# A fused attention and mixture-of-experts kernel: q's high part taken two steps earlier, one residual addition later, weight loads behind the value copies, and three waits of GpSimd left out

## The chip, the cores and the metric

The kernel runs on 1 core of one Trainium2 chip. The metric is the device time of one execution in microseconds (us); lower is better. One execution of the kernel before was also taken by the hardware profiler, and every row below is from that execution.

## The reference

The input x has 4 batches of 512 rows of 256 numbers. Everything is float32.

```python
x = x + attention(layernorm(x), W_qkv, W_out, s)
x = x + experts(layernorm(x), gating_w, w1, b1, w2, b2)

# attention: 8 key/value heads, 4 query heads for each, head size 64
q, k, v = split(layernorm(x) @ W_qkv)
q, k = rope(q), rope(k)            # only a quarter of each head really turns
attn = q @ k.T / 8, masked with -inf where 0 <= q_pos - k_pos < 64
w = softmax([attn, sink s])[..., :-1]
out = (w @ v) @ W_out

# experts: 8, the top 2 for each token, 640 places in each
gates = softmax(x_flat @ gating_w); top 2, normalised
buf[expert, place] = x_flat[token]
h = relu(buf @ w1 + b1); out_e = h @ w2 + b2
out[token] += weight * out_e[expert, place]
```

## The kernel before, in words

**Periods.** The attention is cut into 32 groups: one key/value head of one batch each, with its four query heads. A group has 16 units, one query head times 128 query rows against all 512 keys. The code runs in periods of 16 steps, one unit in a step. `all_periods` (L382) goes through the steps for each engine and calls `step(n, g, j)` four times in each: with n from 0 to 15 for the period's own group, with n - 16 for the group after it, with n + 16 for the group before it and with n + 32 for the one before that. So n = -8 of the next group lies at step 8 of this period, and n = 33 of a group lies at step 1, two periods on. The tables at L357 to L376 say at which n something is done. Every engine runs its own list in this order and stops at any wait that is not met.

**Exact products.** The float32 operands of the matrix products are taken apart in a high part (rounded by ScalarE) and a low part (the difference, by GpSimd), and each product is the sum of three.

**What is done for one group.** In the order of its numbers n:

- TensorE (PE) makes three chunks of the projection: KV (keys and values), Q01 and Q23 (two query heads each). ScalarE (ACT) copies each to `chunk_sb` (`chunk_out`, L879).
- SyncE (SP) copies the quarters that turn against one another into `swap_sb` with two or four DMAs (`swap_halves`, L514).
- GpSimd (POOL) multiplies both with the tables (`turn_parts`, L696 and L698) and adds them (`sum_parts`, L707). ACT takes the high part (`high_part`, L901: `k_hi`, `q_hi`), and POOL the low one (`low_part`, L716: `k_lo`, `q_lo`). For Q23 this is in the group's own period, at step 1 (turn), 2 (sum) and 4 (high and low), and PE needs it for unit 8. For KV and Q01 it is in the second half of the period before.
- The keys' parts are copied to the other 64 partitions by SP (L520, L525). PE turns the values (`turn_v`), ACT copies them to `v_next` (`v_copy`, L887), and SP takes them through DRAM into `v_quads` (`v_out` L532, `v_in` L540).
- In each unit PE makes the scores (L1605), VectorE (DVE) masks them and finds the maximum (L1203), ACT takes the exponentials (L914), and DVE transposes two units at once (L1212, three steps behind the first of them).
- In the next period PE multiplies with the values at steps 4, 6 and 8 (L1631), and DVE divides by the sums (L1232, `heads_sb`). The reciprocals of the sums go through DRAM on SP (`recip_out` L548, `recip_spread` L556, into `recip_wide`). PE multiplies with the output weights (L1663), ACT takes this to `y_sb`, and POOL adds it to x in two halves, the residuals (L750), at n = 33 and 42.
- SP loads the projection weights of the group after the next in three DMAs (`load_w`, L501, L503, L505). ACT and POOL split them (L907, and L663: `w_lo`).

**What else lies in the periods.** In periods 2 to 9 ACT issues a DMA of 662.5 KB that fills one expert's rows in DRAM (L986). In periods 3, 4, 5, 6, 8, 9, 13 to 17 and 22 a tile of 128 rows of a later batch is normalised: ACT writes it at step 2 (L1048), PE turns it at step 4, after ACT's copy of chunk Q01 at step 3; ACT takes its high part at step 5 (L869) and DVE its low part, also at step 5 (L1195). From period 8 on, the batch before is routed to its experts; this is `route`, at numbers r that go on over 8 periods. There POOL computes some small tiles, and at r = 92, 99, 108, 115 and 124 it scatters rows to DRAM (`indirect_dma_start`, L805). r = 99 and 115 are step 3 of the 7th and 8th period of a batch, and each scatter first waits until the reciprocals of a group have landed in `recip_wide`.

Behind the 32 periods, the last batch is routed and the 8 experts run. The change leaves their lists as they are.

## Time and profile before

| | us |
|---|---|
| the runs: median of 3 | 1124.78 |
| the runs: lowest and highest | 1120.2 and 1127.68 |
| the profiled execution | 1124.78 |
| its span in the trace | 1123.0 |
| mean granted TensorE clock, share of full speed | 0.972 |

The span is from the first to the last instruction that the profiler recorded, and the execution's own time is 1.78 us longer. The profiled execution is the median one. Busy times are sums over the instructions of an engine. In a row of a timeline, the first two numbers are start and duration in us; a bracket at its end gives how long the engine had been idle and what released it.

### The profile page before, as it was taken

To read this page: it belongs to the slowest core of one execution; us is meant where nothing else is said; L and a number is where in the kernel's file an instruction comes from. 1 tells how busy PE (TensorE), PEld (TensorE's weight loads), DVE (VectorE), ACT (ScalarE), POOL (GpSimd) and SP (SyncE) were. 2 spreads that over 40 slices of the span, in tenths; PEclk is the share of its full clock that TensorE was granted. 3 is DMA by queue.
4 is the path that set the end of the run, shared out by engine and by line. 5 is a ranking of instruction groups with operands and counts; after the bars stand their busy time and mean duration, and the time that the engine had idled before them with its cause. 6 is when DMAs were issued, how large, how long until landed. Compare 5 with 4: busy or idle time off the path is not lost.

```text
span 1123.0 us, 33679 instructions
## 1 busy us (share of the span) xinstructions
PE 1022.2 (91%) x13525; PEld 791.3 (70%) x13525; DVE 924.3 (82%) x1964; ACT 725.5 (65%) x1796; POOL 753.1 (67%) x671
## 2 busy tenths in 40 slices
PE   6799988899999789999998899999878999999996
PEld 4476666676667566777766567776556899999995
DVE  6898888799999877999997699999784677777773
ACT  4776667677787766778876577877563445445541
POOL 5677777777888779887887788888762233333332
PEclk8899999999999998999999899999899999999999
DMA  4454444445333333344333345344324344444331
GB/s 109 112 123 120 113 118 124 121 131 138 100 89 99 90 94 94 85 122 103 80 94 92 93 109 134 85 108 101 97 63 133 120 120 118 114 101 102 98 77 20
DMA packets 118061, 116.27 MB, mean 104 GB/s; under 512 B 35760, under 2 KB 104432, under 8 KB 117776
## 3 DMA queue, kind: packets, MB, share of 16 engines
q1 hardware_dynamic: 100128, 94.36, 30.8%
q0 software_dynamic: 7296, 8.55, 4.7%
q10 hardware_dynamic: 10480, 11.20, 3.6%
q8 instruction: 107, 1.75, 0.7%
q14 instruction: 50, 0.41, 0.1%
HBM read 74.84 MB, written 21.83 MB: 86 GB/s over the span
## 4 chain that ended last, share of the span: by engine, by line
PE 40%; DVE 23%; POOL 12%; DMA 7%; issue 6%; SPq 5%; ACT 5%; ACTq 0%; POOLq 0%; DVEq 0%
PE bank L1796 10%; DVE probs_ring L1203 10%; PE bank L1631 9%; DVE probs_t L1212 8%; PE bank L1807 6%; PE bank L1605 4%; PE bank L1810 3%; DMA swap_sb<-chunk_sb 3%; DMA recip_wide<-recip_rows 3%; POOL chunk_sb L707 3%; POOL swap_sb L698 3%; SPq L514 3%; ACT probs_ring L914 2%; PE bank L1548 2%; DVE heads_sb L1232 2%
## 5 line engine op out<-in xcount | busy, mean ns | idle before, releaser
L914 ACT ACTIVATE probs_ring<-probs_ring,neg_max 128x512 f32<-128x512 f32 x512 | 365.8, 717 | 182.9 <-DVE neg_max L1203 179.7
L1203 DVE CUSTOM_DVE_ANT_0 probs_ring<-bank,mask,sink_neg 128x512 f32<-128x512 f32 x512 | 359.3, 736 | 42.3 <-PE bank L1605 41.3
L1212 DVE STREAM_TRANSPOSE probs_t<-probs_ring 128x1024 f32<-128x1024 f32 x256 | 318.0, 1242 | 12.7 <-ACT probs_ring L914 12.7
L1631 PE MATMUL bank<-probs_t,v_quads 32*64 32x256 f32 x8192 | 256.3, 391 | 0.2
L1631 PEld LDWEIGHTS bank<-probs_t,v_quads 32*64 32x64 f32 x8192 | 183.5, 136 | 56.1 <-issue 30.0
L1605 PE MATMUL bank<-k_hi,q_hi 64*128 64x512 f32 x512 | 129.6, 497 | 67.5 <-POOL q_lo L716 32.1
L845 POOL DMA_INDIRECT out<-expert_sb,slots x40 | 77.4, 1936 | 154.1 <-DVE expert_sb L1475 132.8
L696 POOL TENSOR_TENSOR chunk_sb<-chunk_sb,rope_sb 128x512 f32<-128x512 f32 (+1 forms) x94 | 120.6, 1283 | 47.3 <-DMA swap_sb<-chunk_sb 40.0
L1605 PEld LDWEIGHTS bank<-k_hi,q_hi 64*128 64x128 f32 x512 | 49.9, 187 | 137.4 <-DVE neg_max L1203 52.2
L1122 ACT ACTIVATE hidden<-bank,b_sb 128x320 f32<-128x320 f32 x128 | 60.4, 524 | 110.7 <-PE bank L1796 107.8
L707 POOL TENSOR_TENSOR chunk_sb<-chunk_sb,swap_sb 128x512 f32<-128x512 f32 (+1 forms) x94 | 120.4, 1281 | 2.6
L698 POOL TENSOR_TENSOR swap_sb<-swap_sb,rope_sb 128x512 f32<-128x512 f32 (+1 forms) x94 | 120.5, 1282 | 0.0
L1663 PE MATMUL bank<-wo_sb,heads_sb 64*128 64x256 f32 x992 | 117.2, 376 | 0.0
L1807 PE MATMUL bank<-w_part,hidden_hi 128*128 128x512 f32 x320 | 114.9, 400 | 0.0
L1605 PE MATMUL bank<-k_lo,q_hi 64*128 64x512 f32 x512 | 105.5, 401 | 0.0
L1605 PE MATMUL bank<-k_hi,q_lo 64*128 64x512 f32 x512 | 105.0, 399 | 0.0
L1663 PEld LDWEIGHTS bank<-wo_sb,heads_sb 64*128 64x128 f32 x992 | 95.1, 186 | 13.9
L914 ACT ACTIVATION_READ_ACCUMULATOR probs_ring<-probs_ring,neg_max 128x1 f32 x512 | 97.4, 190 | 0.0
L1810 PE MATMUL bank<-w_part,hidden_lo 128*128 128x256 f32 x320 | 90.1, 282 | 0.0
L1548 PE MATMUL bank<-xcur,w_hi 64*128 64x512 f32 x496 | 84.9, 408 | 5.4 <-ACT y_sb L923 3.4
L716 POOL TENSOR_TENSOR q_lo<-chunk_sb,q_hi 128x512 fp32r<-128x512 f32 x63 | 80.6, 1280 | 6.4 <-ACT q_hi L901 6.2
L1796 PE MATMUL bank<-slots_hi,w_hi 128*128 128x320 f32 x256 | 79.5, 311 | 2.6 <-ACT hidden L1122 2.6
(202 smaller groups left out, 1813.7 us busy)
## 6 DMA issues: line engine op xcount, KB each, us to landing
v_quads<-v_rows SPq DMA_DIRECT2D x128, 128.0 KB
recip_wide<-recip_rows SPq DMA_DIRECT2D x64, 256.0 KB, 4.7
w_raw<-in_L_ffn_w SPq DMA_DIRECT2D x14, 1024.0 KB, 8.8
swap_sb<-chunk_sb SPq DMA_DIRECT2D x314, 32.0 KB, 3.2
w_raw<-in_L_attn_W_qkv SPq DMA_DIRECT2D x31, 256.0 KB, 2.9
slots<-slot_rows SPq DMA_DIRECT2D x9, 662.5 KB, 4.0
slot_rows<-xn ACTq DMA_DIRECT2D x8, 662.5 KB, 6.5
v_rows<-v_next SPq DMA_DIRECT2D x32, 128.0 KB, 2.1
```

What stands on the lines that cost most here:

```text
L696: nc.gpsimd.tensor_tensor(chunk_sb[c][rows, :], chunk_sb[c][rows, :], rope_sb[rows, 0, :], ALU.mult).then_inc(s_pool, 1)
L698: nc.gpsimd.tensor_tensor(swap_sb[c][rows, :], swap_sb[c][rows, :], rope_sb[rows, 1, :], ALU.mult).then_inc(s_pool, 1)
L707: nc.gpsimd.tensor_tensor(chunk_sb[c][rows, :], chunk_sb[c][rows, :], swap_sb[c][rows, :], ALU.add).then_inc(s_rot, 1)
L914: nc.scalar.activation(probs[(g * UNITS + n) % RING][:, :], probs[(g * UNITS + n) % RING][:, :], ACT.Exp, bias=neg_max[j][:, n:n + 1], sca ...
L1203: nc.vector.tensor_tensor_reduce(probs[(g * UNITS + n) % RING][:, :], SCORE[SCORE_OF[n // 2][n % 2]][:, :], mask[:, L - P - t * P:2 * L - ...
L1212: nc.vector.transpose(probs_t[j][:, :, (h // 2) * (2 * P):(h // 2 + 1) * (2 * P)] .rearrange("p b (h q) -> p h b q", h=2)[:, :, :, t * BLK ...
L1605: ins = nc.tensor.matmul(SCORE[SCORE_OF[n // 2][hh]][:, :], q[half, t * P:(t + 1) * P], k[half, :], start=(m == 0), stop=(m == 2))
L1631: ins = nc.tensor.matmul(PV[a][p * HD:(p + 1) * HD, 0:2 * P], v_quads[j][rows, d, c * HD:(c + 1) * HD], probs_t[j][rows, blk, p * 2 * P:(p ...
L1663: ins = nc.tensor.matmul(PV[a][:, 0:D], heads_sb[rows, a, h * P:(h + 1) * P], wo_sb[rows, (g % NKV) * 2 + h, :], start=(half == 0 and h == ...
L1796: ins = nc.tensor.matmul(banks[4 + 2 * (c % 2) + half][:, 0:HALF], w[:, kc, c * P:(c + 1) * P], a[:, at:at + HALF], start=(kc == 0 and m = ...
L1807: nc.tensor.matmul(FFN2[s][:, :], hidden_hi[:, c, s * P:(s + 1) * P], w2_parts[e % 2][:, c, :, :].rearrange("p t d -> p (t d)"), start=(c ...
L1810: ins = nc.tensor.matmul(FFN2[s][:, 0:D], hidden_lo[:, c, s * P:(s + 1) * P], w2_hi[e % 2][:, c, :], start=False, stop=(c == HC - 1))
```

## The change

It has four parts.

1. `HIGH_AT`: ACT takes q's high part of Q23 at step 2, not at step 4, and k's high part at step 8 of the period before its group's, not at step 9.
2. `RESIDUAL_AT`: POOL adds the first half of the residuals at step 5, not at step 1.
3. SP's list: the copy of k's high part comes ahead of `v_out`, and `load_w` comes behind `v_in`, just ahead of the four DMAs of `swap_halves` for Q23.
4. Three waits of POOL in the routing (at r = 53, 69 and 85, all at step 5 of a period, not for the last batch) are left out.

```diff
-        HIGH_AT = {4: Q23, -7: KV, -6: Q01}
+        HIGH_AT = {2: Q23, -8: KV, -6: Q01}
...
-        Y_FIRST_OUT_AT, Y_OUT_AT, RESIDUAL_AT = 30, 31, (33, 42)
+        Y_FIRST_OUT_AT, Y_OUT_AT, RESIDUAL_AT = 30, 31, (37, 42)
...
                 swap_halves(g + 1, Q01)
+                k_high_twice(g + 1, (g + 1) % 2)
                 v_out(g + 1)
-                k_high_twice(g + 1, (g + 1) % 2)
+                k_low_twice(g + 1, (g + 1) % 2)
+                v_in(g + 1, (g + 1) % 2)
                 if g + 3 < GROUPS:
                     load_w(g + 3, 0)
-                k_low_twice(g + 1, (g + 1) % 2)
-                v_in(g + 1, (g + 1) % 2)
                 swap_halves(g + 1, Q23)
...
-                if r == MEAN_PART_AT and not last:
-                    pool.wait_ge(s_mean_part, b + 1)
-                if r == ONEHOT_AT and not last:
-                    pool.wait_ge(s_chosen, b + 1)
-                if r == PICK_AT and not last:
-                    pool.wait_ge(s_weights, b + 1)
```

From L772 on, the changed kernel's line numbers are 3 to 6 lower.

On ACT, the first steps of period 6, one of those with a tile to normalise, stood like this before (`probs_ring` is an exponential, `chunk_sb` the copy of a chunk, `v_next<-x_sb` the normalised tile, `xcur` its high part):

```order
L879 ACTIVATE chunk_sb<-bank 128x4x4x32 [waits s_qk_lo,s_proj]
L914 ACTIVATE probs_ring,sums<-probs_ring,neg_max 128x512 [waits s_neg_max]
L1048 ACTIVATE v_next<-x_sb,bias_late,rstd_late 128x256 [waits s_v_out,s_late]
L914 ACTIVATE probs_ring,sums<-probs_ring,neg_max 128x512 [waits s_neg_max]
L879 ACTIVATE chunk_sb<-bank 128x4x4x32 [waits s_qk_lo,s_proj]
L914 ACTIVATE probs_ring,sums<-probs_ring,neg_max 128x512 [waits s_neg_max]
L901 ACTIVATE q_hi<-chunk_sb 128x512 [waits s_scores,s_rot]
L914 ACTIVATE probs_ring,sums<-probs_ring,neg_max 128x512 [waits s_neg_max]
L869 ACTIVATE xcur<-bank 128x2x128 [waits s_norm_turned]
```

Now the same stretch of ACT's list reads:

```order
L873 ACTIVATE chunk_sb<-bank 128x4x4x32 [waits s_qk_lo,s_proj]
L908 ACTIVATE probs_ring,sums<-probs_ring,neg_max 128x512 [waits s_neg_max]
L895 ACTIVATE q_hi<-chunk_sb 128x512 [waits s_scores,s_rot]
L1042 ACTIVATE v_next<-x_sb,bias_late,rstd_late 128x256 [waits s_v_out,s_late]
L908 ACTIVATE probs_ring,sums<-probs_ring,neg_max 128x512 [waits s_neg_max]
L873 ACTIVATE chunk_sb<-bank 128x4x4x32 [waits s_qk_lo,s_proj]
L908 ACTIVATE probs_ring,sums<-probs_ring,neg_max 128x512 [waits s_neg_max] x2
L863 ACTIVATE xcur<-bank 128x2x128 [waits s_norm_turned]
```

`q_hi`, which waits for POOL's sum (`s_rot`), has moved ahead of the normalised tile, of the exponential of unit 3, of the copy of chunk Q01 and of the exponential of unit 4.

On SP, the second half of a period stood like this before (`swap_sb` in the last two rows are the four DMAs for Q23):

```order
L532 DMA v_rows<-v_next 128x256 [waits s_v_in0,s_v_next]
L520 DMA k_hi<-k_hi 64x512 [waits s_qk_hi]
L501 DMA w_raw<-in_L_attn_W_qkv 128x2x256 [waits s_w_lo]
L503 DMA w_raw<-in_L_attn_W_qkv 128x2x64
L505 DMA w_raw<-in_L_attn_W_qkv 128x2x64
L525 DMA k_lo<-k_lo 64x512 [waits s_qk_lo]
L540 DMA v_quads<-v_rows 32x4x256 [waits s_pv,s_v_out]
L540 DMA v_quads<-v_rows 32x4x256 x3
L514 DMA swap_sb<-chunk_sb 16x512 [waits s_chunk_out]
L514 DMA swap_sb<-chunk_sb 16x512 x3
```

Now it reads:

```order
L520 DMA k_hi<-k_hi 64x512 [waits s_qk_hi]
L532 DMA v_rows<-v_next 128x256 [waits s_v_in0,s_v_next]
L525 DMA k_lo<-k_lo 64x512 [waits s_qk_lo]
L540 DMA v_quads<-v_rows 32x4x256 [waits s_pv,s_v_out]
L540 DMA v_quads<-v_rows 32x4x256 x3
L501 DMA w_raw<-in_L_attn_W_qkv 128x2x256 [waits s_w_lo]
L503 DMA w_raw<-in_L_attn_W_qkv 128x2x64
L505 DMA w_raw<-in_L_attn_W_qkv 128x2x64
L514 DMA swap_sb<-chunk_sb 16x512 [waits s_chunk_out]
L514 DMA swap_sb<-chunk_sb 16x512 x3
```

The three weight loads have moved from between `k_hi` and `k_lo` to between `v_quads` and `swap_sb`.

On POOL, the first steps of a period stood like this before (`chunk_sb<-chunk_sb,rope_sb 128x512` begins the turn of Q23, `x_sb` is the residual, `64x512` begins the turn of the next group's KV; `s_mean_part` is one of the three waits that the change leaves out):

```order
L696 TENSOR_TENSOR chunk_sb<-chunk_sb,rope_sb 128x512 [waits s_swapped2,s_chunk_out]
L698 TENSOR_TENSOR swap_sb<-swap_sb,rope_sb 128x512
L750 TENSOR_TENSOR x_sb<-x_sb,y_sb 128x2x256 [waits s_residual,s_y_out]
L707 TENSOR_TENSOR chunk_sb<-chunk_sb,swap_sb 128x512 [waits s_pool]
L663 TENSOR_TENSOR w_lo<-w_raw,w_hi 128x768 [waits s_w_hi]
L716 TENSOR_TENSOR q_lo<-chunk_sb,q_hi 128x512 [waits s_qk_hi]
L696 TENSOR_TENSOR chunk_sb<-chunk_sb,rope_sb 64x512 [waits s_swapped0,s_chunk_out,s_mean_part]
```

Now they read:

```order
L696 TENSOR_TENSOR chunk_sb<-chunk_sb,rope_sb 128x512 [waits s_swapped2,s_chunk_out]
L698 TENSOR_TENSOR swap_sb<-swap_sb,rope_sb 128x512
L707 TENSOR_TENSOR chunk_sb<-chunk_sb,swap_sb 128x512 [waits s_pool]
L663 TENSOR_TENSOR w_lo<-w_raw,w_hi 128x768 [waits s_w_hi]
L716 TENSOR_TENSOR q_lo<-chunk_sb,q_hi 128x512 [waits s_qk_hi]
L750 TENSOR_TENSOR x_sb<-x_sb,y_sb 128x2x256 [waits s_residual,s_y_out]
L696 TENSOR_TENSOR chunk_sb<-chunk_sb,rope_sb 64x512 [waits s_swapped0,s_chunk_out]
```

The residual has moved from between the turn and the sum of Q23 to behind its low part, and the wait at the turn of KV is gone.

## Rows read from the trace of the kernel before

**Rows 1.** The page: busy us (share, instructions), and a DMA issue of ACT.
```profile
PE 1022.2 (91%) x13525; PEld 791.3 (70%) x13525; DVE 924.3 (82%) x1964; ACT 725.5 (65%) x1796; POOL 753.1 (67%) x671
...
slot_rows<-xn ACTq DMA_DIRECT2D x8, 662.5 KB, 6.5
```
**Rows 2.** Line L1203 by itself: count, ns, first and last start.
```profile
L1203 DVE CUSTOM_DVE_ANT_0 probs_ring<-bank,mask,sink_neg x512: 701/745/758, 22.6 to 841.2; 128x512 f32<-128x512 f32 x171
```
**Rows 3.** Waits of DVE: us in total, times, longest us.
```profile
DVE probs_ring L1203 <- PE bank L1605: 41.3, 22, 6.3
...
DVE xcur L1195 <- ACT xcur L869: 17.1, 12, 3.0
DVE probs_t L1212 <- ACT probs_ring L914: 12.7, 13, 1.7
```
**Rows 4.** Waits of POOL.
```profile
POOL chunk_sb L696 <- DMA swap_sb<-chunk_sb: 40.0, 24, 7.8
POOL slot_rows L805 <- DMA recip_wide<-recip_rows: 29.9, 6, 6.2
...
POOL chunk_sb L696 <- DVE xn L424: 6.4, 3, 2.3
```
**Rows 5.** Line L696 alone from 90 to 310 us: what ended its idle time.
```profile
  DMA swap_sb<-chunk_sb: 23.1, 9
```
**Rows 6.** Timeline of POOL, period 5 (starts at 149.64) and the start of 6.
```profile
153.91 1.28 POOL L696 TENSOR_TENSOR chunk_sb<-chunk_sb,rope_sb 128x512 f32<-128x512 f32 x1 [3.73 <-DMA swap_sb<-chunk_sb]
...
156.38 1.28 POOL L750 TENSOR_TENSOR x_sb<-x_sb,y_sb 128x512 f32<-128x512 f32 x1
...
179.73 1.29 POOL L696 TENSOR_TENSOR chunk_sb<-chunk_sb,rope_sb 128x512 f32<-128x512 f32 x1 [3.22 <-DMA swap_sb<-chunk_sb]
```
**Rows 7.** Timeline of ACT, period 5.
```profile
154.14 0.59 ACT L1048 ACTIVATE v_next<-x_sb,bias_late,rstd_late 128x256 f32<-128x256 f32 x1
...
155.81 0.71 ACT L914 ACTIVATE probs_ring<-probs_ring,neg_max 128x512 f32<-128x512 f32 x1
...
158.93 0.63 ACT L901 ACTIVATE q_hi<-chunk_sb 128x512 fp32r<-128x512 f32 x1 [2.32 <-POOL chunk_sb L707]
...
160.17 0.36 ACT L869 ACTIVATE xcur<-bank 128x256 fp32r<-128x256 f32 x1
```
**Rows 8.** Timeline of DVE, period 5.
```profile
156.28 1.25 DVE L1212 STREAM_TRANSPOSE probs_t<-probs_ring 128x1024 f32<-128x1024 f32 x1
160.57 0.42 DVE L1195 TENSOR_TENSOR xcur<-bank,xcur 128x256 fp32r<-128x256 f32 x1 [3.04 <-ACT xcur L869]
```
**Rows 9.** Timeline of SP's DMA issues, period 5.
```profile
167.33 0.35 SPq L532 DMA_DIRECT2D v_rows<-v_next  x1
...
168.45 0.62 SPq L501 DMA_DIRECT2D w_raw<-in_L_attn_W_qkv  x1
...
170.21 0.51 SPq L525 DMA_DIRECT2D k_lo<-k_lo  x1
...
172.82 3.66 SPq L514 DMA_DIRECT2D swap_sb<-chunk_sb  x4
```
**Rows 10.** Lines L532 and L514 alone, each: us from issue to landing.
```profile
DMA to landing us min/median/max: 1.7/2.1/4.2
...
DMA to landing us min/median/max: 1.9/3.2/5.3
```
**Rows 11.** Timeline of POOL, period 24 (starts at 642.6) and the start of 25.
```profile
643.07 1.29 POOL L696 TENSOR_TENSOR chunk_sb<-chunk_sb,rope_sb 128x512 f32<-128x512 f32 x1
...
657.63 1.29 POOL L716 TENSOR_TENSOR k_lo<-chunk_sb,k_hi 64x512 fp32r<-64x512 f32 x1
...
666.06 1.30 POOL L696 TENSOR_TENSOR chunk_sb<-chunk_sb,rope_sb 128x512 f32<-128x512 f32 x1
```
**Rows 12.** Timeline of DVE, period 13.
```profile
375.27 1.25 DVE L1212 STREAM_TRANSPOSE probs_t<-probs_ring 128x1024 f32<-128x1024 f32 x1 [1.38 <-ACT probs_ring L914]
```
**Rows 13.** Timeline of POOL, period 15, the second with such a scatter.
```profile
420.26 1.00 POOL L805 DMA_INDIRECT slot_rows<-xn,scatter_idx  x1 [4.67 <-DMA recip_wide<-recip_rows]
```

## The prediction

> **What bounds the kernel now.** I read the page first: DVE is busy 82% of the span, the highest share of an engine but PE [rows 1]. Line L1203, which opens each unit on DVE, begins at 22.6 and for the last time at 841.2 us [rows 2]: 818.6 us for 511 units, or 25.6 us for a period of 16. That is the stage the change touches, with 32 periods. A period in which DVE hardly idles is shorter: POOL's work for Q23 begins at 643.07 and one period on at 666.06, 23.0 us [rows 11]. So DVE sets the pace, and what can be won or lost is DVE's idle time. The waits of DVE tell who makes it: PE's scores 41.3 us, ACT's high part of a normalised tile 17.1 us in 12 periods, ACT's exponentials 12.7 us [rows 3]. POOL's waits tell what lies behind these: the swap DMAs 40.0 us in 24 waits, the reciprocals ahead of a scatter 29.9 us in 6, and a removed wait (L424 releases it) 6.4 us in 3 [rows 4]. In the early periods the swap DMA is the late one: 23.1 us in 9 waits between 90 and 310 us [rows 5].
>
> I call x the time from a period's first L1203 to POOL's first instruction for Q23. In period 5 it is 153.91 - 149.64 = 4.3 us, all of it a wait for the swap DMA, and one period on it is again late by a wait of 3.22 us [rows 6]. The circle is 179.73 - 153.91 = 25.8 us long: POOL's sum releases ACT's q_hi, behind which stands the tile's high part L869; L869 releases DVE's L1195 after 3.04 us of idleness [rows 7, 8]; DVE's later units release the value copy, and SP's list leads from there to the swap of the next Q23 [rows 9]. In these periods this circle sets the time, and no engine's busy share shows it.
>
> **ACT's order in the early periods.** q_hi waits for the sum. Before, the tile, two exponentials and a chunk copy were done ahead of it, in the shadow of that wait: from 154.14 to 155.81 + 0.71 = 156.52, so 2.4 us [rows 7]. Now they stand behind it. The sum itself comes 1.3 us earlier, since the residual (1.28 us) is no longer ahead of it [rows 6]. L869 and then L1195 come 2.4 - 1.3 = 1.1 us later, counted from x. Besides, the transposition of units 2 and 3, which DVE begins 156.28 - 149.64 = 6.6 us into the period [rows 8], needs the exponential of unit 3, now behind q_hi: three POOL instructions of 1.25 (3.75), q_hi 0.6 and the exponential 0.7 give x + 5.1. From x = 1.5 on DVE idles there, in any period.
>
> **SP's order.** Three things make the swap of Q23 start later. k_hi now comes ahead of the exponential of unit 9 and so of the value copy: up to 0.6 us (q_hi of the same kind takes 0.63 [rows 7]); at least nothing, if ACT was idle. The copy out and the copy in were 3.5 us apart, filled with the weight loads (167.33 to 170.21 + 0.6). Now the copy in must wait for the landing of the copy out, 2.1 us [rows 10], with only k_lo in between, and the loads (168.45 to 170.21, 1.76 us) come behind: 2.1 + 2.0 + 1.8 = 5.9 us from copy out to swap, against 172.82 - 167.33 = 5.5 [rows 9]. So 0.4 more. With ACT's 1.1 the swap starts up to 2.1 us later from x.
>
> The Trainium skill, DMA: Bandwidth & Descriptors, in its rules for kernel authors, says to issue a DMA early and to wait late, so that its fixed cost is overlapped. Before, the loads did that for the copy out; the changed list undoes it. By that rule SP's part is a loss, as the rows make it.
>
> **Sum, costs.**
> (a) Periods 3, 4, 5, 6, 8 and 9 have a tile and a late swap. Each grows by 1.1 (only ACT's order; the swap then lands no later) to 2.1 us (the whole circle). The swap in period 5 took 3.66 us to issue, beside the DMA of 662.5 KB, which lands after 6.5 us [rows 1, 9]; if that alone decides, the low end holds. I take 1.8, nearer to the circle: 10.8, bounds 6.6 and 12.6.
> (b) Periods 1, 2 and 10 have a late swap and no tile. Period 10 has a wait of the kind of rows 5, and lies over the limit of 1.5 even with x as it is. I take 4 for the three, bounds 0 and 6.
> (c) From 11 on x was short. The new circle of POOL and SP: from POOL's first instruction to the end of k_lo 657.63 + 1.29 - 643.07 = 15.9 [rows 11]; k_lo and the copy in 172.82 - 170.21 = 2.6; the loads 1.8 [rows 9]; four swaps, the last issued about 1.9 us behind the first and landing 1.9 at least, 3.8 [rows 10]. Together 24.1 us, with the residual still in it. Before it was 22.3, under the shortest period of 23.0; now it is over it. In the four or five periods near 23 x rises by about 1 us each until DVE idles. I take 5, bounds 0 and 8.
>
> **Sum, gains.**
> (d) In period 0 Q23 needs no late DMA, and in period 7 there is no tile: q_lo comes 1.3 us or more earlier. I take -2.5, bounds -4 and 0.
> (e) Of the waits left out only that at r = 85 cost much: 2.1 us each in periods 13, 21 and 29. It made POOL late for Q01 and ACT with it, and DVE idled 1.38 us in period 13 [rows 12]. Three such are -4.2; x is higher there now, so -3, bounds -4.2 and 0. The scatter has its own wait for the weights.
> (f) In periods 12, 20 and 28 POOL has small tiles ahead of q_lo; -1 for the three, bounds -1.5 and 0.
>
> The six periods with a scatter at step 3 gain nothing: POOL waited 4.67 us for the reciprocals with everything for Q23 but the low part done [rows 13], and the residual lay in that shadow. Now it lies behind q_lo, but PE and DVE are behind there anyway. Cost 0, bounds -1 and 3 for all six.
>
> 10.8 + 4 + 5 - 2.5 - 3 - 1 = 13.3 us. The profiled execution took 1124.78 us, the median itself: 1138 us.
>
> **The rivals.**
> *It cancels.* The swap still lands when the large DMA lets it, x stays as it is after period 10: (a) 6.6, (b) 1, (c) 0, against gains of 6.5. That gives 1.1, so 1126 us. For it: the swap's stretched issue of 3.66 us. Against it: SP's list had no gap from 167.33 to the swap in period 5 [rows 9].
> *q's low part was the bound.* DVE waited 41.3 us for scores, and the reciprocals explain 29.9 of them [rows 3, 4]; if the other 11.4 go by half (5.7), with -4.2 of (e), and -2 of (d), and the swap lands as before because SP is seldom late, it is 1113 us. For it: two changes shorten just this chain. Against it: where x is over 1.5, ACT stands still at step 2.
> *The loads hold up the swap.* They put three transfers ahead of it on SP's own queue. If the swap lands 5.3 us after its issue, the longest of rows 10, and not 1.9 to 3.2, the circle of (c) is over 25.6 us, the mean period, and the 15 periods from 11 on without such a scatter lose some 0.8 us more each: 1150 us. It decides once POOL waits for the swap in every period.
>
> The Trainium skill, the same page, on queues, rings and completion order, says that a DMA engine takes turns between the queue rows that have work, and takes descriptors of one row in order. By the first half ACT's large DMA and SP's swap share the engines (the cancelling rival's ground); by the second the loads, on the swap's own row, are taken first (the last rival's). No row shows a load right ahead of a swap.
>
> **How the numbers follow.** My forecast has 0.50, with a range of its own from 1129 to 1146; cancelling has 0.24, the low part 0.16, the held-up swap 0.10. A measurement of this kernel can tell about 1% (11 us) from no change, so "slower" begins at 1136. Of the forecast two thirds lie above that, 0.33, and with the last rival slower has 0.43. The rest of the forecast and the cancelling case give 0.41 within 1%. Faster has 0.16. The range from 1113 to 1148 reaches to both neighbours.
>
> **What would show it.** Right: POOL's wait for the swap DMA grows well over 40 us; ACT's wait for POOL at q_hi now stands ahead of the tile; DVE's waits for exponentials, at the transposition of units 2 and 3, rise over 12.7 us; period 5 is 27 us or longer; the waits for L424 are gone. Wrong: x at or below 4.3 in period 5 and below 1.5 after 11, and period 5 at 26 us or less. Then SP's list had slack that I did not see, or the swap lands earlier with less around it.

## The result, and the profile after

The changed kernel takes 1173.68 us (median of 3, 1171.0 to 1178.11) against 1124.78: a ratio of 1.0445, with a 95% interval from 1.0369 to 1.0522. It is slower by 49 us, where I forecast 13 and a range up to 23. Measured once more beside later runs of the kernel before, it took 1163.06 us (1.0381, 1.0344 to 1.0419). Of the four executions of the first experiment (e1), one took 1405.44 us at a mean granted clock of 0.65, and it is left out of that experiment's ratio.

The page after answers to [rows 1]. DVE is busy 16.6 us longer, with the same 1964 instructions. That is odd for a change that adds no work to DVE, and it is the first sign of what I missed.

```profile
PE 1039.6 (89%) x13525; PEld 798.5 (68%) x13525; DVE 940.9 (80%) x1964; ACT 727.1 (62%) x1796; POOL 753.9 (64%) x671
```

Line L1197 (L1203 before) by itself, as in [rows 2]; its columns are count, least, median and longest ns, first and last start. The last unit begins at 883.4 us, not at 841.2.

```profile
L1197 DVE CUSTOM_DVE_ANT_0 probs_ring<-bank,mask,sink_neg x512: 699/744/753, 22.7 to 883.4; 128x512 f32<-128x512 f32 x171
```

The waits after, as in [rows 3, 4], with two of ACT and PE: us in total, times, longest.

```profile
POOL chunk_sb L696 <- DMA swap_sb<-chunk_sb: 61.5, 29, 7.9
ACT q_hi L895 <- POOL chunk_sb L707: 71.7, 39, 3.8
DVE probs_ring L1197 <- PE bank L1599: 48.7, 36, 5.3
DVE probs_t L1206 <- ACT probs_ring L908: 39.7, 30, 3.9
PE bank L1506 <- ACT chunk_sb L873: 22.1, 10, 4.2
DVE xcur L1189 <- ACT xcur L863: 10.1, 12, 0.9
```

The wait for the swap DMA rose from 40.0 to 61.5, and that for the exponentials at the transposition from 12.7 to 39.7, as forecast. The wait at DVE's part of the tile fell from 17.1 to 10.1, since DVE now comes late to it. PE's wait for the copy of a chunk at the turn of the tile is new, and DVE's wait for scores rose from 41.3 to 48.7.

I took the length of each period from the starts of its first unit on DVE in both traces, and summed it by the terms of the prediction (us, the 31 differences between first units):

| term | periods | before | after | difference | forecast |
|---|---|---|---|---|---|
| (a) tile and late swap | 3, 4, 5, 6, 8, 9 | 153.8 | 170.4 | +16.7 | +10.8 |
| (b) late swap, no tile | 1, 2, 10 | 75.2 | 75.9 | +0.7 | +4 |
| (d) | 0, 7 | 53.4 | 53.0 | -0.5 | -2.5 |
| (c) the new circle | 11, 16 to 19, 24 to 27 | 215.8 | 224.6 | +8.8 | +5 |
| (f) | 12, 20, 28 | 72.1 | 73.2 | +1.1 | -1 |
| (e) the removed wait at r = 85 | 13, 21, 29 | 76.0 | 92.8 | +16.8 | -3 |
| scatter at step 3 | 14, 15, 22, 23, 30 | 148.6 | 146.8 | -1.8 | 0 |
| behind the last unit's start | | 281.8 | 286.8 | +5.0 | 0 |

Each column is one execution. What the rows can tell is seen from three kernels of the experiments (e8, e9, e10) whose whole time is that of before: their rows differ from those of before by up to 2.9 us for (a), 2.8 for (c), 1.1 for (e) and 4.1 for the scatter periods.

Where (a) comes from shows in period 5, which begins at 155.9 us. The same engines as in [rows 6 to 9], in the kernel after: start, duration, what ended the idle time.

```profile
159.69 1.29 POOL L696 TENSOR_TENSOR chunk_sb<-chunk_sb,rope_sb 128x512 f32<-128x512 f32 x1 [3.23 <-DMA swap_sb<-chunk_sb]
...
162.30 1.26 POOL L707 TENSOR_TENSOR chunk_sb<-chunk_sb,swap_sb 128x512 f32<-128x512 f32 x1
...
187.59 1.29 POOL L696 TENSOR_TENSOR chunk_sb<-chunk_sb,rope_sb 128x512 f32<-128x512 f32 x1 [3.08 <-DMA swap_sb<-chunk_sb]
```
```profile
163.60 0.63 ACT L895 ACTIVATE q_hi<-chunk_sb 128x512 fp32r<-128x512 f32 x1 [3.09 <-POOL chunk_sb L707]
164.13 0.58 ACT L1042 ACTIVATE v_next<-x_sb,bias_late,rstd_late 128x256 f32<-128x256 f32 x1
...
167.22 0.36 ACT L863 ACTIVATE xcur<-bank 128x256 fp32r<-128x256 f32 x1
```
```profile
165.46 1.25 DVE L1206 STREAM_TRANSPOSE probs_t<-probs_ring 128x1024 f32<-128x1024 f32 x1 [2.81 <-ACT probs_ring L908]
```
```profile
174.37 0.51 SPq L520 DMA_DIRECT2D k_hi<-k_hi  x1
175.34 0.35 SPq L532 DMA_DIRECT2D v_rows<-v_next  x1
175.74 0.50 SPq L525 DMA_DIRECT2D k_lo<-k_lo  x1
177.78 1.75 SPq L540 DMA_DIRECT2D v_quads<-v_rows  x4
179.58 0.43 SPq L501 DMA_DIRECT2D w_raw<-in_L_attn_W_qkv  x1
...
181.08 4.00 SPq L514 DMA_DIRECT2D swap_sb<-chunk_sb  x4
```

The circle is 187.59 - 159.69 = 27.9 us, against 25.8. q_hi and the tile stand behind POOL's sum, and L863 begins 7.5 us behind POOL's start (L869 before: 6.3). SP stands still for 1.5 us between k_lo's copy and v_in (176.24 to 177.78), until the copy out has landed, and the weight loads come only behind that.

PE stood idle in the same period for ACT's copy of the chunk:

```profile
165.96 0.33 PE L1506 MATMUL bank<-identity,v_next 128*128 128x128 f32 x1 [3.09 <-ACT chunk_sb L873]
```

From 166 to 170 us the mean granted clock was then 0.57, so that most of these 4 us went by at 1.2 GHz; in the rest of the period it was 1.00. The prediction has no term for this. Over the whole execution the mean is 0.953, against 0.972 before, and PE is busy 17.4 us longer with the same instructions. It was 0.88 to 0.94 in each of the six tile periods (before: 1.00 in five and 0.94 in one), and 0.89, 0.89 and 0.94 in periods 13, 21 and 29 (before: 1.00).

Where (e) comes from is in period 13, in DVE's rows and POOL's:

```profile
380.95 1.24 DVE L1390 TENSOR_TENSOR slot_base<-slot_base,batch_total 128x8 f32<-128x8 f32 x1
382.11 0.41 DVE L1189 TENSOR_TENSOR xcur<-bank,xcur 128x256 fp32r<-128x256 f32 x1
...
383.36 0.17 DVE L1397 TENSOR_TENSOR full<-slot_f,slot_end 128x8 f32<-128x8 f32 x1
383.56 3.68 DVE L1398 SCALAR_TENSOR_TENSOR scatter_idx<-full,slot_f 128x8 uint32<-128x8 f32 x1
```
```profile
380.90 1.26 POOL L696 TENSOR_TENSOR chunk_sb<-chunk_sb,rope_sb 64x512 f32<-64x512 f32 x1
382.13 1.26 POOL L698 TENSOR_TENSOR swap_sb<-swap_sb,rope_sb 64x512 f32<-64x512 f32 x1
383.47 1.28 POOL L707 TENSOR_TENSOR chunk_sb<-chunk_sb,swap_sb 64x512 f32<-64x512 f32 x1
384.71 1.27 POOL L696 TENSOR_TENSOR chunk_sb<-chunk_sb,rope_sb 128x512 f32<-128x512 f32 x1
385.95 1.26 POOL L698 TENSOR_TENSOR swap_sb<-swap_sb,rope_sb 128x512 f32<-128x512 f32 x1
```

`scatter_idx` has 8 elements for each partition. It begins 0.09 us behind POOL's L707 and ends at 387.24, when the last of three POOL instructions without a gap ends (387.21). `slot_base` ends at 382.19, when the first of two such (L696, 382.16) ends, though L698 begins at 382.13. The same tile in the kernel before, and there POOL's idle time in front of it:

```profile
L1404 DVE SCALAR_TENSOR_TENSOR scatter_idx<-full,slot_f x4: 166/166/166, 363.8 to 872.6; 128x8 uint32<-128x8 f32 x4
```
```profile
364.56 1.27 POOL L696 TENSOR_TENSOR chunk_sb<-chunk_sb,rope_sb 64x512 f32<-64x512 f32 x1 [2.29 <-DVE xn L424]
```

The wait that the change removed kept POOL idle from 362.3 to 364.6, and in just this stretch DVE did its small operations. `picked`, just ahead of them, met POOL's q_lo: it took 1.12 to 1.16 us in periods 13, 21 and 29 and 0.22 only in the last batch. So the trace of before already showed an operation of DVE held by POOL, and I had not looked at it.

```profile
L428 DVE TENSOR_TENSOR picked<-onehot,prefix x4: 218/1128/1155, 361.2 to 871.9; 128x64 f32<-128x64 f32 x4
```

In the three periods after, `slot_base` takes 1.24 each instead of 0.15, `scatter_idx` 3.68, 1.20 and 1.20 instead of 0.17, and the weights (L424) 3.43 and 1.06 in two of them instead of 0.19: together 13.0 us more, while `picked` takes 1.0 less in sum. That was a reading of two columns side by side, and so the first thing to test.

### The profile page after: what moved, and what is told of

Its sections match the earlier page's. It is cut to its first block, busy times and chain, and to the rows that moved or that the text cites. A ratio compares the mean times of both kernels' runs of the same rounds, so it can differ in the third digit from the quotient of the medians.

```text
span 1170.2 us, 33679 instructions
## 1 busy us (share of the span) xinstructions
PE 1039.6 (89%) x13525; PEld 798.5 (68%) x13525; DVE 940.9 (80%) x1964; ACT 727.1 (62%) x1796; POOL 753.9 (64%) x671
## 4 chain that ended last, share of the span: by engine, by line
PE 35%; POOL 19%; SPq 11%; DMA 11%; DVE 11%; ACT 6%; issue 6%; another core or an unknown queue 0%; ACTq 0%; POOLq 0%; DVEq 0%
PE bank L1790 10%; PE bank L1801 6%; PE bank L1625 6%; DMA swap_sb<-chunk_sb 5%; POOL chunk_sb L696 5%; POOL swap_sb L698 5%; SPq L514 4%; POOL chunk_sb L707 4%; DVE probs_ring L1197 4%; PE bank L1599 3%; PE bank L1804 3%; SPq L540 3%; DVE probs_t L1206 3%; ACT probs_ring L908 3%; DMA v_rows<-v_next 3%
## 5 line engine op out<-in xcount | busy, mean ns | idle before, releaser
L1197 DVE CUSTOM_DVE_ANT_0 probs_ring<-bank,mask,sink_neg 128x512 f32<-128x512 f32 x512 | 359.0, 734 | 50.9 <-PE bank L1599 48.7
L1206 DVE STREAM_TRANSPOSE probs_t<-probs_ring 128x1024 f32<-128x1024 f32 x256 | 317.3, 1240 | 39.7 <-ACT probs_ring L908 39.7
L1625 PE MATMUL bank<-probs_t,v_quads 32*64 32x256 f32 x8192 | 261.1, 397 | 0.0
L1625 PEld LDWEIGHTS bank<-probs_t,v_quads 32*64 32x64 f32 x8192 | 183.7, 138 | 61.0 <-issue 35.6
L1599 PE MATMUL bank<-k_hi,q_hi 64*128 64x512 f32 x512 | 132.3, 509 | 58.8 <-DVE neg_max L1197 34.0
L696 POOL TENSOR_TENSOR chunk_sb<-chunk_sb,rope_sb 128x512 f32<-128x512 f32 (+1 forms) x94 | 120.5, 1281 | 61.8 <-DMA swap_sb<-chunk_sb 61.5
L707 POOL TENSOR_TENSOR chunk_sb<-chunk_sb,swap_sb 128x512 f32<-128x512 f32 (+1 forms) x94 | 120.1, 1278 | 4.9
L698 POOL TENSOR_TENSOR swap_sb<-swap_sb,rope_sb 128x512 f32<-128x512 f32 (+1 forms) x94 | 120.3, 1280 | 0.0
L895 ACT ACTIVATE q_hi<-chunk_sb 128x512 fp32r<-128x512 f32 x64 | 40.1, 627 | 73.1 <-POOL chunk_sb L707 71.7
```

The source lines that it names most:

```text
L696: nc.gpsimd.tensor_tensor(chunk_sb[c][rows, :], chunk_sb[c][rows, :], rope_sb[rows, 0, :], ALU.mult).then_inc(s_pool, 1)
L698: nc.gpsimd.tensor_tensor(swap_sb[c][rows, :], swap_sb[c][rows, :], rope_sb[rows, 1, :], ALU.mult).then_inc(s_pool, 1)
L707: nc.gpsimd.tensor_tensor(chunk_sb[c][rows, :], chunk_sb[c][rows, :], swap_sb[c][rows, :], ALU.add).then_inc(s_rot, 1)
L1197: nc.vector.tensor_tensor_reduce(probs[(g * UNITS + n) % RING][:, :], SCORE[SCORE_OF[n // 2][n % 2]][:, :], mask[:, L - P - t * P:2 * L - ...
L1206: nc.vector.transpose(probs_t[j][:, :, (h // 2) * (2 * P):(h // 2 + 1) * (2 * P)] .rearrange("p b (h q) -> p h b q", h=2)[:, :, :, t * BLK ...
L1599: ins = nc.tensor.matmul(SCORE[SCORE_OF[n // 2][hh]][:, :], q[half, t * P:(t + 1) * P], k[half, :], start=(m == 0), stop=(m == 2))
```

## The experiments

The runs are numbered in the order in which they were made. In each, the time is compared with the kernel before on the same chip. "Periods 13, 21, 29" and the like are sums of lengths as in the table. A ratio of 1.01 is 11.2 us. "Shared-port theory" in the expectations is my short name for what period 13 suggests: a small operation of DVE with its operands in SBUF is held while POOL runs tensor operations.

### The removed waits

The kernel before with the three waits left out, and the changed kernel with them put back:

```diff
-                if r == PICK_AT and not last:
-                    pool.wait_ge(s_weights, b + 1)
```

**e1**

> The kernel before with the three waits of GpSimd (r = 53, 69, 85) left out and nothing else. Shared-port theory: without the wait at r = 85 POOL runs its two-input tensor ops back to back just while DVE does the small two-input ops of the routing, and these are held up to 3.7 us each, as in the changed kernel; periods 13, 21 and 29 grow by 4 to 7 us each, and the whole by 12 to 20 us, to 1137 to 1145 us; the scatter_idx instructions of DVE (0.166 us each before) have a longest of over 1 us. My step (e) as predicted: POOL and then ACT are earlier for Q01, the whole is 3 us faster (1122), the small DVE ops stay at 0.15 to 0.2 us. Third: the long periods 13, 21, 29 need the higher x of the changed lists too, then this kernel is within 3 us of before.

Measured: 1133.36 us, 1.0084 (1.0062 to 1.0107), 9 us more. Periods 13, 21 and 29 add up to 88.5 us, +12.5; periods 0 to 10 are 1.9 us shorter and the others 1.7 longer, both within what such sums vary.

**e2**

> The changed kernel with the three waits of GpSimd put back. Shared-port theory: the 16.9 us that periods 13, 21 and 29 lost go, and it is 1154 to 1158 us; the rest of the loss (17 us in periods 0 to 10, 8 us from 11 on without these three) stays, since it is the q_hi order and SP's list. If the loss in 13, 21 and 29 came from the moved residual or from the circle of POOL and SP, it stays at 1170 to 1174 us.

Measured: 1158.03 us, 1.0309 (1.0289 to 1.0329). Periods 13, 21 and 29 fall from 92.8 to 80.4, and (a) and (c) stay at +16.3 and +10.8. So my step (e) had the wrong sign, in either company, and the other 34 us have other causes. These include the 4.4 us that the three periods keep: `slot_base` still takes 1.24 and 1.25 us in two of them, since the other parts of the change put POOL's operations beside it. In the trace of the first of these, period 13 reads:

```profile
363.90 3.66 DVE L1398 SCALAR_TENSOR_TENSOR scatter_idx<-full,slot_f 128x8 uint32<-128x8 f32 x1
```
```profile
363.81 1.27 POOL L707 TENSOR_TENSOR chunk_sb<-chunk_sb,swap_sb 64x512 f32<-64x512 f32 x1
365.04 1.26 POOL L696 TENSOR_TENSOR chunk_sb<-chunk_sb,rope_sb 128x512 f32<-128x512 f32 x1
366.28 1.26 POOL L698 TENSOR_TENSOR swap_sb<-swap_sb,rope_sb 128x512 f32<-128x512 f32 x1
```

Which wait it was: the next leaves out those at r = 53 and 69 and keeps r = 85.

**e8**

> The kernel before with the waits at r = 53 and 69 left out and the one at r = 85 kept. Shared-port theory, by the placed ops: at r = 69 (periods 12, 20, 28) POOL is behind and the onehot, chosen and slot_end ops of DVE keep 0.17 to 0.2 us in the profile of the kernel with all three out, so the loss of 9.5 us there was r = 85 alone, and this kernel is within 2 us of before, 1122 to 1126 us. Rival: the loss is spread over the three waits, then 1127 to 1130 us.

Measured: 1123.11 us, 1.0002 (0.9984 to 1.0019). Leaving out the other two costs nothing, so the loss is r = 85.

Now one other wait at another place, with the three left out:

```diff
                 q, rows = g * CHUNKS + c, rows_of(c)
                 pool.wait_ge(s_pool, before_group + (q - Q23 + 1) * ROT_STEPS)
+                if c == KV and g % 8 == 6 and g > 8:
+                    pool.wait_ge(s_routed, g // 8)
```

**e7**

> The kernel before with the three waits of GpSimd left out, and one other wait put in: in periods 13, 21 and 29 POOL's sum for KV (step 6) waits until DVE's scatter_idx is there (s_routed), which it does not need. Shared-port theory (a small two-input op of DVE is held until POOL's chain of tensor ops breaks): scatter_idx falls from 3.66 us in period 13 to at most the rest of one POOL instruction, 0.2 to 1.3 us, while slot_base, which lies beside L696 and L698, stays at 1.25; POOL idles under 1 us there; period 13 is 27 to 28 us instead of 30.7 and the whole 1125 to 1130. Rival (DVE was late because of the data, semaphores or the order of its list, not POOL's activity): scatter_idx stays at 3.7 us or POOL waits that much, and period 13 stays over 30 us, 1133 us.

Measured: 1134.79 us, 1.0097 (1.0057 to 1.0137). Of DVE and POOL in period 13:

```profile
366.57 0.17 DVE L1400 SCALAR_TENSOR_TENSOR scatter_idx<-full,slot_f 128x8 uint32<-128x8 f32 x1
...
367.06 3.59 DVE L424 TENSOR_TENSOR xn<-gates,top_sum 128x32 f32<-128x32 f32 x1
```
```profile
366.88 1.26 POOL L709 TENSOR_TENSOR chunk_sb<-chunk_sb,swap_sb 64x512 f32<-64x512 f32 x1 [0.48 <-DVE scatter_idx L1400]
368.11 1.26 POOL L696 TENSOR_TENSOR chunk_sb<-chunk_sb,rope_sb 128x512 f32<-128x512 f32 x1
369.34 1.26 POOL L698 TENSOR_TENSOR swap_sb<-swap_sb,rope_sb 128x512 f32<-128x512 f32 x1
```

`scatter_idx` is free, as the shared-port theory said. The time was not: I had not seen that L424 stands right behind it, and the same chain of three caught that one. The miss of the total speaks for the mechanism, since another instruction with other data was held for the same 3.6 us (3.59 and 3.52 us in periods 13 and 29, and 1.07 in period 21). The last of this group has the same diff with `s_weights` in the place of `s_routed`.

**e9**

> As e7 (the three waits left out, one wait put in at POOL's sum for KV in periods 13, 21 and 29), but this one waits for DVE's weights (s_weights), so the last of the small two-input ops is behind it. In e7 scatter_idx fell to 0.17 us and the weights, 0.3 us behind it in DVE's list, took 3.59 us in its place. Shared-port theory: now the weights too take 0.19 us, slot_base alone stays at 1.25 (it lies beside L696 and L698), POOL idles 0.8 to 1.1 us in place of the 2.3 of the kernel before, periods 13, 21 and 29 add up to 76 to 80 us, and the whole is 1121 to 1126 us. Rival (the wait at r = 85 helped by something else, such as the order in which SP or ACT are released): 1131 to 1136 as in e1 and e7.

Measured: 1120.17 us, 1.0007 (0.9985 to 1.003); periods 13, 21 and 29 add up to 76.8 us against 76.0. POOL waits 1 us at its sum, and DVE's row is short again:

```profile
362.80 1.27 POOL L709 TENSOR_TENSOR chunk_sb<-chunk_sb,swap_sb 64x512 f32<-64x512 f32 x1 [0.99 <-DVE xn L424]
```
```profile
L424 DVE TENSOR_TENSOR xn<-gates,top_sum x4: 191/192/192, 362.5 to 869.0; 128x32 f32<-128x32 f32 x4
```

With all three waits gone and POOL idle 2.9 us in all for this one, the 9 us are back. So the data had been there all along, and what counted was that POOL ran no tensor operation beside `scatter_idx` and the weights. `slot_base` still takes 1.23 to 1.26 us here, with next to no effect on the sum.

### ACT's order and the residual

`HIGH_AT` alone, with both of its entries:

```diff
-        HIGH_AT = {4: Q23, -7: KV, -6: Q01}
+        HIGH_AT = {2: Q23, -8: KV, -6: Q01}
```

**e3**

> The kernel before with the HIGH_AT table of the changed kernel alone (q_hi of Q23 at step 2, k_hi at step 8); residual, SP's list and waits as before. ACT-order theory: q_hi, behind which the tile's high part and the exponential of unit 3 now stand, waits for a sum that still comes behind the residual, so the shadow of 2.4 us is lost without the 1.3 us that the moved residual gives back: the periods 1 to 10 lose 2 to 2.5 us each, 20 us (1145), DVE's wait for exponentials at L1212 and L1206's counterpart rises well over 12.7 us, and q_hi waits over 60 us for POOL. SP theory (it is the order of SP's list that makes the circle late): this kernel is within 5 us of before (1120 to 1130).

Measured: 1156.59 us, 1.0307 (1.0263 to 1.035), 34 us. DVE's wait at the transposition is 51.3 us and q_hi's for POOL 82.3. The six tile periods grow by 24.3 us, 4 each, and the whole is 12 us above what I had put down. Its KV entry alone:

**e10**

> The kernel before with k_hi at step 8 (HIGH_AT -8: KV) and nothing else. HIGH_AT as a whole cost 33 us, and q_hi with the residual 17. If k_hi is a cost of its own, since it stands ahead of the exponential of unit 9 and of the value copy and waits for POOL's sum for KV, SP's copy out starts 0.6 us or more later and this kernel loses 5 to 12 us: 1127 to 1134. If the 33 us come from q_hi alone (ahead of the tile, and without the earlier sum that the moved residual gives), this one is within 3 us of before, 1119 to 1125.

Measured: 1122.25 us, 1.0006 (0.9984 to 1.0029). k_hi's place costs nothing by itself. Then the residual alone, `RESIDUAL_AT` (37, 42):

**e5**

> The kernel before with the first half of the residuals at step 5 (RESIDUAL_AT 37, 42) and nothing else. HIGH_AT alone cost 33 us and SP's list 21, but both together with this move 34: so in that company the move is worth some 20 us, or the two losses overlap. If the move is a gain of its own (POOL's sum, ACT's q_hi and POOL's q_lo 1.3 us earlier in each period), this kernel is at 1110 to 1120 us, and PE's waits for q_lo at L1605 (44.3 and 32.1 us) fall by a quarter or more. If it only gives back what HIGH_AT loses, it is within 3 us of before, 1121 to 1127.

Measured: 1129.61 us, 1.0067 (1.0039 to 1.0095), and neither case held: 7.5 us slower. The tile periods gain 2.4 us, but (c) loses 3.0, POOL waits 35.6 us for the reciprocals instead of 29.9, and periods 13, 21 and 29 lose 3.2. In these the residual now runs at step 5, beside DVE's `slot_base`, which takes 1.25 us again, with the wait at r = 85 in place. This fits the 3.2 us and is not shown to be their cause: in e9 `slot_base` was held as long, and the three periods grew by 0.8. The earlier sum hardly reached PE, because q_hi stayed at step 4: POOL's q_lo waits 16.0 us for it (6.2 before), and PE's waits for q_lo are 42.8 and 24.7 us, against 44.3 and 32.1. Both moves of Q23 together:

**e6**

> The kernel before with q_hi of Q23 at step 2 and the residual at step 5; k_hi, SP's list and the waits as before. My terms (a) and (b) say that ACT's order costs 1.1 us in each of six to nine periods, 7 to 10 us, less 2.5 in periods 0 and 7: 1130 to 1133 us. If q_hi's order is the larger part of the loss seen with HIGH_AT alone, 1135 to 1142, periods 1 to 10 longer by 1 to 1.5 us each. If k_hi at step 8 was the costly half of HIGH_AT, this kernel is at 1120 to 1126 us.

Measured: 1138.46 us, 1.0153 (1.0125 to 1.0181), 17 us; the six tile periods grow by 11.9, 2.0 each, not 1.1. With q_hi at step 2 the residual's move is worth 17 us (e3 costs 34, and k_hi nothing), though by itself it costs 7.5. Then with q_hi one step later:

```diff
-        HIGH_AT = {4: Q23, -7: KV, -6: Q01}
+        HIGH_AT = {3: Q23, -7: KV, -6: Q01}
```

**e13**

> As e6 (residual at step 5, k_hi and SP's list as before) but q_hi at step 3: behind the tile and the exponentials of units 2 and 3, still ahead of the copy of chunk Q01 and the exponential of unit 4. Theory: in e6 the tile and the exponential of unit 3 were taken out of the shadow of q_hi's wait, so DVE stood at the transposition of units 2 and 3, and PE at the turn of the tile. With q_hi behind both, DVE's wait for exponentials (29.1 us in e6) falls to 15 to 22, L869 comes 1.3 us earlier than in e6, periods 0 to 10 add up to 281 to 285 us instead of 295.1, and the whole is 1126 to 1131 us, near the residual's own cost of 8. Rival: the chunk copy behind q_hi is what counts (PE waited 15.5 us for it in e6); then periods 0 to 10 stay over 290 us and the whole over 1134.

Measured: 1125.40 us, 1.0037 (1.0019 to 1.0055); periods 0 to 10 add up to 282.0 us, against 295.0 in e6 and, in the kernel before, 282.4. DVE's wait fell below the 15 to 22 us that I expected. The waits of DVE with q_hi at step 2, and then at step 3:

```profile
DVE probs_t L1212 <- ACT probs_ring L914: 29.1, 21, 2.6
```
```profile
DVE probs_t L1212 <- ACT probs_ring L914: 12.7, 16, 1.8
```

So the price is the tile and the exponential of unit 3, taken from in front of a wait to behind it. The copy of the chunk, still behind q_hi, is not: PE still waits 9.1 us for it (16.3 with q_hi at step 2), and periods 0 to 10 are as short as before. With the stall the lower clock goes too: in the six tile periods it was 0.88 to 0.94 in five in e6, and here 0.94 in two and 1.00 in four. How much of the 2.0 us a period is the lower clock, no run separates.

### SP's list

The whole reordering alone, as in part 3 of the change:

**e4**

> The kernel before with SP's list of the changed kernel alone (k_hi copy, v_out, k_lo copy, v_in, weight loads, swap for Q23); HIGH_AT, residual and waits as before. ACT-order theory: 0.4 to 1 us in each of some 9 early periods and little after: 1128 to 1133 us. SP theory: most of the 25 us outside of periods 13, 21 and 29, so 1140 to 1150 us, and POOL's wait for the swap DMA rises from 40.0 to over 55 us. If SP's list had slack, 1125 and the wait stays near 40.

Measured: 1145.03 us, 1.0177 (1.0137 to 1.0218), 20 us; POOL's wait for the swap is 72.5 us. That is the SP theory's size. With the loads behind v_in alone (v_out still ahead of k_hi):

**e11**

> The kernel before with the weight loads behind the copy in of the values (v_in), just ahead of the swap for Q23, and the rest of SP's list as it was: v_out, then the copy of k_hi, then that of k_lo. The whole reordering cost 21 us. Theory 'k_hi ahead of v_out': v_out starts 1.2 us later in each circle only because of k_hi's copy, and from v_out to the swap it is 5.6 us against 5.5; then the loads alone cost under 5 us, 1121 to 1126. Theory 'loads' (the lost cover of the copy out, as in my prediction, and the loads on the swap's own queue right ahead of it): 12 us or more, 1133 to 1142 us.

Measured: 1137.36 us, 1.0145 (1.0106 to 1.0184), 16 us. With k_hi's copy ahead of v_out alone:

**e14**

> The kernel before with the copy of k_hi ahead of v_out in SP's list and nothing else; the weight loads stay ahead of the copy of k_lo. The whole reordering cost 21 us, the loads alone 15. SP has slack here: the loads end about when POOL's k_lo does (16.3 us behind POOL's start of Q23 in periods 1 to 10), so what k_hi's copy takes ahead of v_out (0.5 us and up to 0.6 of waiting) is paid in full only if the loads fill that slack: then about 0.3 us in each of 25 periods, 1126 to 1130 us. If v_out's start hardly matters, 1120 to 1125.

Measured: 1124.61 us, 1.0022 (1.0003 to 1.0041), 2.5 us. So the loads are nearly all of it, and the theory of e11 that k_hi's copy was the costly part fell. The rows of the run with the loads behind say what they had hidden in, in period 5:

```profile
171.67 1.28 POOL L716 TENSOR_TENSOR k_lo<-chunk_sb,k_hi 64x512 fp32r<-64x512 f32 x1
```
```profile
170.83 0.35 SPq L532 DMA_DIRECT2D v_rows<-v_next  x1
171.35 0.57 SPq L520 DMA_DIRECT2D k_hi<-k_hi  x1
172.98 0.50 SPq L525 DMA_DIRECT2D k_lo<-k_lo  x1
173.81 1.76 SPq L540 DMA_DIRECT2D v_quads<-v_rows  x4
175.61 0.43 SPq L501 DMA_DIRECT2D w_raw<-in_L_attn_W_qkv  x1
```

SP stands from 171.9 to 172.98, until POOL's k_lo ends (171.67 + 1.28 = 172.95). It is this wait that the loads had covered here, and not the landing of the copy out, which I had priced. Over the whole execution SP waits 61.6 us for POOL's k_lo, against 11.0 before, and 3.7 us for the landing, against 2.1. (In the changed kernel, where v_out itself goes out later, the landing does hold, 19.6 us in all: rows of period 5 above.) Averaged over periods 1 to 10, counted from POOL's start for Q23, k_lo's copy goes out at 16.7 us before and 16.2 here, but the swap at 19.6 before and 20.9 here: 1.3 us later. In periods 16 to 20 and 24 to 28 it is 19.8 and 20.3.

What k_hi's place adds to the list (`HIGH_AT` with -8 for KV and the whole reordering):

**e17**

> The kernel before with k_hi at step 8 and the whole reordering of SP's list; q_hi of Q23, the residual and the waits as before. Open from the runs so far: in the nine periods of term (c), 11, 16 to 19 and 24 to 27, the changed kernel loses 8.8 to 10.8 us, of which SP's list alone gives 4.5 and q_hi with the residual 0.7. If k_hi's place and SP's list work together (k_hi on ACT ahead of the value copy, then its copy ahead of v_out), these nine periods add up to 223 to 227 us, against 215.8 before and 220.4 with the list alone, and the whole is 1.020 to 1.026 of before. If k_hi's place is neutral here too, 219 to 222 us and 1.015 to 1.020; then the other 4 us need the residual at step 5 beside SP's list.

Measured: 1142.35 us, 1.0167 (1.0126 to 1.0209), no more than the list alone; the nine periods add up to 222.2 us, 1.9 more than with the list alone, within what this sum varies. k_hi's place is neutral here too.

If the loads are free inside a wait, they can be hidden better still, in SP's idle time ahead of v_out:

```diff
                 swap_halves(g + 1, Q01)
+                if g + 3 < GROUPS:
+                    load_w(g + 3, 0)
                 v_out(g + 1)
                 k_high_twice(g + 1, (g + 1) % 2)
-                if g + 3 < GROUPS:
-                    load_w(g + 3, 0)
```

**e15**

> The kernel before with the weight loads moved the other way: ahead of v_out, in the stretch in which SP stands idle between the swap for Q01 and v_out. Theory: SP's chain is copy of k_lo (which waits for POOL's k_lo, done 16.3 us behind POOL's start of Q23), v_in, swap for Q23; loads behind it lengthen the circle, loads ahead of it hide in a wait. Before, k_lo's copy left 0.4 us (periods 1 to 10) and 0.7 us (later) after POOL's k_lo, since the loads ended only then. Now it leaves at once: 0.3 to 0.6 us a circle, where the swap is the late one, 1114 to 1120 us, and POOL's wait for the swap falls under 35 us. Rival (only the order at the end of the list matters, and before had nothing to gain): within 2 us of before.

Measured: 1117.78 us, 0.9973 (0.9952 to 0.9995), 3 us faster than before. In period 5, k_lo's copy leaves 0.03 us behind POOL's k_lo (166.99 + 1.27 = 168.26):

```profile
159.49 0.40 SPq L501 DMA_DIRECT2D w_raw<-in_L_attn_W_qkv  x1
...
166.11 0.34 SPq L532 DMA_DIRECT2D v_rows<-v_next  x1
166.63 0.54 SPq L520 DMA_DIRECT2D k_hi<-k_hi  x1
168.29 0.51 SPq L525 DMA_DIRECT2D k_lo<-k_lo  x1
```

But POOL's wait for the swap is 36.3 us, not under 35, and the swap goes out only 0.2 us earlier on the mean of either stretch, not 0.3 to 0.6. The swap itself now waits for ACT's copy of its chunk: in period 5 v_in's last issue ends at 170.95, ACT's copy at 171.36 (170.79 + 0.57), and the swap goes out at 171.39. Over all periods SP's wait for these copies is 54.8 us, against 46.8 before. The gain is at the edge of what these executions can tell.

**e16**

> e15 and e9 together: loads ahead of v_out, the waits at r = 53, 69 and 85 left out, and POOL's sum for KV in periods 13, 21 and 29 waiting for DVE's weights. If both gains are there and add, 1112 to 1118 us; the small two-input ops of DVE but slot_base stay at 0.2 us. If e9's 1120 was nothing but scatter, it is where e15 is.

Measured: 1119.25 us, 0.9983 (0.9961 to 1.0004). That is above the 1118 of the case in which both gains add: nothing is seen to add to the loads ahead of v_out.

### The changed kernel again

**e12**

> The changed kernel once more. In its first profile the time behind the last unit was 286.8 us, against 281.8 before and 278.6 to 280.7 in the eight experiments, though nothing of the change lies there. If this was one execution, the time behind the last unit is now 278 to 282 us, and the periods add up as before: 299, 93, 147 and 298 us for periods 0 to 10, the three at 13, 21 and 29, the five with a scatter at step 3, and the others. If the change does something to the last part, it is 285 us or more again. The median: 1168 to 1175 us.

Measured: 1163.06 us, below what I expected. The groups are as before: 300.3 us for periods 0 to 10, 92.8 for 13, 21 and 29, 144.9 with a scatter, 300.1 for the others. The time behind the last unit is 280.7, so the +5.0 of the table was that one execution's and not the change's. In that execution PE stood idle for 2.96 us until 931.58, for ACT's copies of `hidden`, and from 930 to 938 us the mean granted clock was 0.57. The profiled execution before has a stall of this kind too (2.24 us until 887.36) with the clock at 1.00, and this one has neither in that stretch. What held ACT until 930.58 stays open. The groups are those of the execution of 1167.61 us, the longest of the four, and why the median fell by 10 us stays open too.

This second execution also shows what three POOL instructions without a gap (385.55 to 389.28) can do in another way:

```profile
385.63 1.22 DVE L1398 SCALAR_TENSOR_TENSOR scatter_idx<-full,slot_f 128x8 uint32<-128x8 f32 x1
386.77 1.30 DVE L1407 SCALAR_TENSOR_TENSOR top_sum<-gate_sum,top_sum 128x4 f32<-128x4 f32 x1
```

Here `scatter_idx` is let go at the end of the first, and then `top_sum` and the weights (388.32, 1.01 us) are held for one each. DVE comes out at the same place, the end of the chain, but it was not one operation that was held to it.

## Why the prediction was wrong

The steps, in the order of the prediction:

- **(e), the removed waits: -3 forecast, +16.8 there.** This is the step that failed: I took the wait at r = 85 for a pure cost, and leaving it out loses time. By itself that costs 12.5 us in these periods (e1), and putting it back gives 12.4 (e2), so some 15 of the 36 us that were missing are this step's. The other 4.4 us in the same periods belong to the other parts of the change (SP's list alone 2.5, the residual alone 3.2). I priced the wait as 2.1 us of POOL's time each, and asked only who waits for POOL. I did not ask what ran beside POOL's idle time. DVE's small operations did, and without it some of them were held, each for one or for three POOL instructions. The runs e1, e7, e8 and e9 show it. My upper bound of 0 was wrong with it, since it allowed a removed wait no loss at all.
- **(a), tile periods: +10.8 forecast, +16.7 there,** over its bound of 12.6. Right in mechanism, and the term that was mis-sized is ACT's order, with the clock put at nothing. I had 1.1 us a period for it and 0.7 for SP's; e6 shows 2.0, and with SP's list and k_hi's place added (e2) it is 16.3 / 6 = 2.7, so 0.7 for these, as forecast (SP's list alone gives 6.7 / 6 = 1.1, e4). L863 came 1.3 us later from POOL's start, near the 1.1. What the step left out is that DVE now stands at the transposition as well and meets the later units' scores late (L1197 waits 0.42 us at 172.21 in period 5), and that the granted clock falls: it does so in the kernels with q_hi at step 2 (e3, e6, e2 and the changed one), and in no tile period with SP's list alone (e4). How the excess over 1.1 us divides between the two is not shown. The swap goes out 2.0 us later from POOL's start in periods 1 to 10 (21.6 for 19.6), within the 2.1 of the text.
- **(b) +0.7 for 4, (d) -0.5 for -2.5, (f) +1.1 for -1.** Small, within 3.3 us each, and hardly more than such rows vary. The gain of the moved residual is there only beside q_hi at step 2 (17 us, e3 against e6); alone, the move costs 7.5 us, where I had only gains and a zero. (f) has the sign wrong, in part for the reason of (e): in the trace after, `chosen` takes 1.30 us in period 20 and `slot_end` 1.24 in period 28, instead of 0.19 and 0.17.
- **(c), the new circle: +5 forecast, +8.8 there,** a little over its bound of 8. The circle that I worked out was 24.1 us. Measured from POOL's start to POOL's next, over periods 16 to 20 and 24 to 28, it is 24.9 after, 24.7 with the loads alone behind, and 24.0 before, with x up from 0.7 to 1.8. In the sum, the stretch from the first swap's issue to POOL's start is 3.8 us; behind period 10, where POOL waited for it, it is 4.5. SP's list alone gives 4.5 of the 8.8 (e4), the loads alone 4.7 (e11). q_hi with the residual adds 0.7 (e6), and k_hi's place nothing of its own (e17). The 2 to 4 us that are left may lie with the residual at step 5 beside the new list (alone, it adds 3.0, e5). This was not tried by itself, and the same sum differs by up to 2.8 us between kernels as fast as before, so it stays open.
- **The rivals.** "It cancels" and "q's low part was the bound" fall: the swap's wait rose, and the whole is no faster. "The loads hold up the swap" names the part of SP's list that counts, and the wrong reason. The traces have no landing times for the swap of Q23; those of [rows 10] are of the other swaps. But where POOL waited for it, POOL's start tells: it came 2.6 us in the median behind the last of the four issues (25 periods), against 2.7 before (19) and 2.4 with the loads alone behind (27), and never the 5.3 us of the rival. So the swap did not queue behind the loads.
- **The sum of the parts.** Measured alone, q_hi with the residual (17 us), SP's list (20) and the removed waits (9) make 46 us, against 49 and 42 for the changed kernel in its two measurements. So no large part of the loss lies in their company.

**A rule that I had not weighed.** Rows first: `slot_base` (two operands in SBUF) takes 1.24 us beside POOL and 0.15 beside an idle one, and L1189, with one operand in a bank, takes 0.41 in either case. The Trainium skill, SBUF — State Buffer, in "Who interferes with whom", says that a DVE instruction with two SBUF inputs contends with a GpSimd instruction that reads SBUF. The same page, in its summary of rules for kernel authors, says that the second one to issue fully blocks "until the first finishes". The trace agrees on who is held, and for `slot_base` on how long. The 3.68 us of `scatter_idx`, over three POOL instructions of 1.26 to 1.28, differ, and the measurement decides. In all the traces 11 of the `scatter_idx` and weights began while POOL's KV sum (L707) ran with two more instructions right behind it: 7 were held over all three and 4 over the first alone. What decides between the two is open.
